# Two-layer cross-attention on one core: scores and row maxima in the two row halves of the TensorE array, maxima issued in pairs of heads

## The chip, the cores and the metric

The kernel runs on one core of a Trainium2 chip. The metric is the device time of one execution in microseconds (us). Engines are named as in the profile: PE is TensorE (PEld its weight loads), DVE is VectorE, ACT is ScalarE, POOL is GpSimd, SP is SyncE, which issues most DMAs here.

## What is computed

Two cross-attention layers are applied one after the other to x of shape (8, 256, 320), with a context of shape (8, 256, 512), 20 heads of 16 columns. The first layer attends to 77 text rows and to the other 179 rows with separate softmaxes and adds the two; the second attends to 252 text rows, and to 4 image rows with a softmax that also contains a cosine term.

```python
# layer 0
q = heads(x @ Wq.T); k = heads(text @ Wk.T); v = heads(text @ Wv.T)
out = attend(q, k, v) + attend(q, k_ip, v_ip)          # softmax(q k / 4) v, twice
x = out @ Wo.T + bo + x
# layer 1
probs_t = softmax(q @ k_t / 4); text_out = probs_t @ v_t
qsem = l2norm(probs_t @ text_ehs); sem = qsem @ l2norm(ip_ehs)
probs_ip = softmax(q @ k_ip / 4 + 0.5 * sem) * spatial_mask
out = (text_out + probs_ip @ v_ip) @ W_out + b_out + x
```

## The kernel before

The work is cut into 16 units: units 0 to 7 are the eight batches in the first layer, 8 to 15 the same in the second. A unit has 10 slots, one for each pair of heads; a slot q = 10 u + j is the unit of the order. `plan(u, j)` lists what happens in a slot, and the programs of all five engines walk the same list, so a table at the top of the file (`PACE`, `MAXH`, ...) sets the order everywhere.

While unit u is attended, two other units are under way: the projections of unit u + 2 ("bg", in three pieces a slot, L388 and L415), and the row maxima of the scores of unit u + 1 ("max", L482), which are needed before its scores can be shifted. A slot holds on TensorE, in this order: the scores of the next pair (L505, two 512-column matmuls, one for each half of the keys), one head of maxima, in even slots the weighing of four heads ("weigh", L537 to L551: four tiles of 32 columns side by side, tile_position (0, 32 j)), in the second layer two quadratic forms ("quad", L519), then the pieces of projection with the other maxima between them, and in even slots four or two transposes ("back", L560). The maxima are dealt three to a slot in slots 0 to 5 and two in slot 6.

Precision is kept by splitting each operand into a rounded high part and a low part. A head has 48 rows in the packed tiles: 16 high, 16 low, 16 high again. In `QP` and `KP` head a of a pair lies in rows 48 a to 48 a + 47; `QP` of a head is zero in the other head's rows, so a maximum contracts over 96 rows (`KROWS`) and the scores over 100 (`QROWS`), the last four being the shift rows (the maxima, high and low) against rows of `ind`. The queries and keys reach these tiles through DRAM (L756, L764), the shift rows by DMAs of one row each (`rows_out`, L780): the high ones from ScalarE's queue in the first layer, the low ones from SyncE's.

PSUM has eight banks. `pPV` is kept for the weighing; the other seven are a pool. `take` gives out, when the program is built, the free bank that was given back first, and makes TensorE wait until whoever reads it is through: VectorE for maxima (dv_mx), for quads (dv_y), for transposes (dv_nb); ScalarE for scores (ac_exp, the exponential at L876); both for projections (ac_bg, dv_bg) and for the transposed output (ac_ot, dv_ot).

ScalarE does, in the order of the list, the rounded exponentials of the scores (second layer, L866), the copy of pPV after a weighing, and the exponentials proper (L876). VectorE reduces each head's maxima (first layer 128x154 and 128x358, second 128x504 and a copy of four columns), multiplies the quads (L1116), computes the low parts (L1001) and normalizes (L1129 to L1147). GpSimd subtracts in the second layer (L1352).

The first slots of units 0 and 1 (`LATE_MAX`) and the slots before unit 0 (u = -1) put the maxima behind the projections.

Of the kernel before, what the change touches and what calls it, by code (L numbers as in the profile page):

```python
# [7 lines left out]
F32 = mybir.dt.float32  # L8
# [6 lines left out]
U = 2 * B  # L15
# [7 lines left out]
KROWS = 96  # L23
QROWS = 100
# [15 lines left out]
MAXH = (3, 3, 3, 3, 3, 3, 2, 0, 0, 0)  # L40
MAXF = (3, 3, 3, 3, 2, 2, 2, 2, 0, 0)
# [40 lines left out]
def plan(u, j):  # L82
# [17 lines left out]
    many = MAXF if u < 0 else MAXH  # L100
    heads = [("max", u + 1, h) for h in range(sum(many[:j]), sum(many[:j + 1]))] if u + 1 < U else []
    first, rest = heads[:1], heads[1:]
# [3 lines left out]
    scores = [("scores", q + 1)] if u >= 0 and q + 1 < U * NP else []  # L106
    weigh = [("weigh", *divmod(q // 2 - 1, NG))] if q >= 2 and q % 2 == 0 else []
    weigh += [("weights", q + 1)] if scores else []
    if u >= B:
        out += scores + weigh + [("quad", q, 0)] + first + [("quad", q, 1)]  # L110
    elif (u, j) in LATE_MAX:
        out += scores + weigh
        rest = heads
    else:
        out += scores + first + weigh
    out += pieces[0] + pieces[1] + rest[:1] + pieces[2] + rest[1:]
# [58 lines left out]
def build(nc, xT, cT, cipT, fs, Wq0, Wk0, Wv0, Wki0, Wvi0, Wo0, bo0,  # L175
          Wq1, Wk1, Wv1, Wki1, Wvi1, Wo1, bo1, ident_d, ind_d, hm_d, outT):
    with ExitStack() as ctx:
# [18 lines left out]
        wk = sb("wk", [128, 2, EC, C], F32R)  # L196
        wv = sb("wv", [128, 2, EC, C], F32R)
# [4 lines left out]
        ind = sb("ind", [4, 2, S], F32R)  # L202
# [12 lines left out]
        P = sb("P", [128, PR, 2, 2 * S])  # L215
        Y = sb("Y", [128, PR, 2, 2 * S])
# [5 lines left out]
        G = [flat(wk)[:, 0:896], flat(wk)[:, 896:1792], flat(wv)[:, 0:896]]  # L222
        PH = [[flat(wv)[:, 896 + 512 * i:896 + 512 * i + 512] for i in range(2)], [flat(w)[:, at:at + 512] for w, at in ((wv, 1920), (wk, 1792))]]
# [25 lines left out]
        Y_flat = Y[:, :, :, :].rearrange("p a b c -> p (a b c)")  # L249
# [16 lines left out]
        def stage(tile, at, n):  # L266
            return flat(tile)[:, at:at + n * C].rearrange("p (k n) -> p k n", n=C)

        sq0, sk0 = stage(Y, 0, KC), stage(Y, KC * C, EC)
        ski0, sv0, svi0 = stage(P, 0, EC), stage(P, EC * C, EC), stage(O2, 0, EC)  # L270
        so0 = stage(Y, 0, KC)
        wki1, wvi1 = stage(Y, 0, EC), stage(Y, EC * C, EC)
        sq1, sk1 = stage(Y, 0, KC), stage(Y, KC * C, EC)
        sv1 = stage(Y, 0, KC), stage(Y, (KC + EC) * C, 1)
# [25 lines left out]
        po_y, po_rn, po_ip, po_set, po_v, po_big, po_q, po_mix = (sem(f"po_{n}") for n in ("y", "rn", "ip", "set", "v", "big", "q", "mix"))  # L300
# [12 lines left out]

        ind_f = flat(P)[0:4, 2 * EC * C:2 * EC * C + S], flat(Y)[0:4, 2 * EC * C:2 * EC * C + S]

        def ind_ready(u):
            u = u if u < 2 else B + u % 2 if u >= B else u % 2
            return l_ind[u], 16

        def rows_landed(u):  # L320
            return l_m[u % 2], 64 * (u // 2 + 1) if u < B else 256 + 32 * ((u - B) // 2 + 1)
# [11 lines left out]
        def tensor_program(_):  # L333
# [142 lines left out]
            def maximum(u, h):  # L476
                i, j, a = u % 2, h // 2, h % 2
                bank = take("mx", u * H + h)
                pe.wait_ge(*pack_landed(u, h // 8))
                pe.wait_ge(po_set, 2 + u % 2)  # L480
                for sc in range(2):
                    made = mm(bank[:, sc * S:sc * S + S], QP[i][0:KROWS, j, a, sc * 128:sc * 128 + 128],  # L482
                              KP[i][0:KROWS, j, :], start=True, stop=True)
                made.then_inc(pe_mx, 1)
                give(bank)
# [191 lines left out]
            for u in range(-1, U):  # L677
# [30 lines left out]
                if u < 0:  # L708
                    scores(0)
# [940 lines left out]
```

## Time and profile before

| | us |
|---|---|
| median of 3 runs | 806.78 |
| lowest, highest | 806.47, 809.67 |
| the profiled execution, its own time | 808.78 |
| its span, first to last instruction | 806.8 |
| busy: PE, DVE, ACT, POOL | 762.5, 567.9, 425.4, 403.0 |
| a unit of the first layer (unit 4, scores of slot 0 to slot 0 of unit 5) | 38.4 |
| a unit of the second layer (unit 11) | 54.8 |

The profile shows one execution. Matmuls are pipelined, so their durations overlap; what one costs is read from the distance between starts. A line of the timeline gives the start, the length and the number of instructions merged in it. Slots are found by their scores (L505): the scores at the head of slot j belong to the pair of slot j + 1.

### The profile page before, as it was taken

How to read it: one execution, taken by the hardware profiler on the slowest of the kernel's cores; microseconds unless marked ns; L12 is line 12 of the kernel's file. 1: busy time of each engine (PE TensorE's matmuls, PEld its weight loads, DVE VectorE, ACT ScalarE, POOL GpSimd, SP SyncE). 2: the span in 40 equal slices, each digit the busy share in tenths (PEclk: the TensorE clock that was granted, in tenths of full speed). 3: DMA queues.
4: the chain of work that ended last, by engine and by line, in shares of the span. 5: the costliest groups of instructions: out<-in, count | busy, mean ns of one | idle time of the engine just before them, and what ended most of it. 6: DMA issues, size and time to landing. Idle time of an engine off the chain costs nothing.

```text
span 806.8 us, 17013 instructions
## 1 busy us (share of the span) xinstructions
PE 762.5 (95%) x6246; PEld 616.4 (76%) x6246; DVE 567.9 (70%) x1575; ACT 425.4 (53%) x915; POOL 403.0 (50%) x297
## 2 busy tenths in 40 slices
PE   5889999999999999999999999999999999988896
PEld 5777788888788877777877778788777787766574
DVE  5357465757576676858768778698697797686745
ACT  5234646464637373646475565555655655555551
POOL 6511222020202040405568887787779778779763
PEclk9999999999999999999999999999999999999999
DMA  9854735654537372735252354153162332400010
GB/s 282 257 165 145 190 111 154 201 169 138 164 113 200 113 202 75 205 94 158 94 146 91 96 144 152 46 157 115 49 190 70 103 118 66 126 1 17 20 34 17
DMA packets 102514, 100.65 MB, mean 125 GB/s; under 512 B 9752, under 2 KB 101664, under 8 KB 102432
## 3 DMA queue, kind: packets, MB, share of 16 engines
q1 hardware_dynamic: 101952, 99.24, 42.2%
q8 instruction: 50, 0.82, 0.4%
q10 hardware_dynamic: 480, 0.33, 0.2%
q14 instruction: 32, 0.26, 0.1%
HBM read 61.65 MB, written 36.74 MB: 122 GB/s over the span
## 4 chain that ended last, share of the span: by engine, by line
PE 71%; DVE 9%; issue 5%; DMA 5%; ACT 4%; POOL 3%; SPq 2%; POOLq 0%; DVEq 0%; ACTq 0%
PE pB L388 19%; PE pB L519 12%; PE pB L482 8%; PE pB L505 7%; PE pB L603 5%; PE pPV L546 4%; PE pPV L541 4%; PE pPV L551 3%; DMA KP<-k0d 3%; PE pPV L537 2%; PE pB L560 2%; POOL Y L1352 2%; DVE m_sb L1101 2%; PE pB L415 1%; ACT P L876 1%
## 5 line engine op out<-in xcount | busy, mean ns | idle before, releaser
L1352 POOL TENSOR_TENSOR Y<-P,wv 128x512 f32<-128x512 f32 x120 | 157.0, 1326 | 106.6 <-ACT P L876 106.5
L1116 DVE TENSOR_TENSOR Y<-pB,Y 128x512 f32<-128x512 f32 x160 | 109.0, 686 | 67.3 <-PE pB L519 56.8
L482 PE MATMUL pB<-KP,QP 96*128 96x256 f32 x640 | 129.1, 287 | 5.0 <-DMA KP<-k0d 3.6
L1329 POOL TENSOR_TENSOR klo<-xin,khi 128x256 fp32r<-128x256 f32 x18 | 13.2, 756 | 232.1 <-ACT khi L787 232.1
L482 PEld LDWEIGHTS pB<-KP,QP 96*128 96x128 f32 x640 | 106.7, 191 | 17.8 <-issue 5.4
L1101 DVE TENSOR_REDUCE m_sb<-pB 128x2 f32<-128x504 f32 x160 | 108.0, 676 | 6.5 <-PE pB L482 5.3
L505 PE MATMUL pB<-QP,KP 100*128 100x512 f32 x320 | 109.8, 422 | 1.9 <-DMA QP<-mlo 1.5
L876 ACT ACTIVATE P<-pB 128x512 f32<-128x512 f32 x160 | 86.5, 597 | 39.5 <-PE pB L505 29.7
L866 ACT ACTIVATE wv<-pB 128x512 fp32r<-128x512 f32 x120 | 66.8, 591 | 67.3 <-PE pB L505 66.0
L876 ACT ACTIVATE P<-pB,ln 128x512 f32<-128x512 f32 x160 | 101.1, 691 | 0.0
L787 ACT ACTIVATE Vs<-pPV 128x512 f32<-128x512 f32 (+1 forms) x80 | 39.3, 492 | 104.7 <-PE pPV L541 71.3
L1099 DVE TENSOR_REDUCE m_sb<-pB 128x2 f32<-128x358 f32 x160 | 83.2, 520 | 0.0
L388 PE MATMUL pB<-cc,wki 128*128 128x256 f32 (+3 forms) x576 | 80.8, 273 | 0.1
L1098 DVE TENSOR_REDUCE m_sb<-pB 128x2 f32<-128x154 f32 x160 | 49.8, 312 | 41.7 <-PE pB L482 41.0
L519 PE MATMUL pB<-wv,wk 128*128 128x512 f32 x250 | 76.7, 410 | 2.5 <-DVE ipS L1103 2.4
L388 PEld LDWEIGHTS pB<-cc,wki 128*128 128x128 f32 (+1 forms) x576 | 70.6, 172 | 6.5 <-issue 4.1
L388 PE MATMUL pB<-wvi,cc 128*128 128x320 f32 (+1 forms) x384 | 68.0, 314 | 1.0 <-POOL wvi L1342 1.0
L388 PE MATMUL pB<-khi,wq 128*128 128x256 f32 (+1 forms) x288 | 56.7, 292 | 9.9 <-DVE wq L1001 8.5
L388 PEld LDWEIGHTS pB<-wvi,cc 128*128 128x128 f32 x384 | 60.0, 190 | 7.1 <-issue 4.5
L1375 POOL TENSOR_TENSOR rn<-n,mhalf 128x8 f32<-128x8 f32 (+2 forms) x17 | 57.1, 3358 | 15.6 <-DVE n L1147 15.6
L519 PEld LDWEIGHTS pB<-wv,wk 128*128 128x128 f32 x250 | 44.3, 189 | 21.1 <-issue 10.3
L505 PEld LDWEIGHTS pB<-QP,KP 100*128 100x128 f32 x320 | 50.8, 191 | 6.3 <-DMA QP<-mlo 2.3
(175 smaller groups left out, 1477.3 us busy)
## 6 DMA issues: line engine op xcount, KB each, us to landing
QP<-q0d SPq DMA_DIRECT2D x64, 192.0 KB, 4.1
KP<-k0d SPq DMA_DIRECT2D x64, 192.0 KB, 4.2
c_sb<-in_cT SPq DMA_DIRECT2D x16, 512.0 KB, 5.3
q0d<-qhi SPq DMA_DIRECT2D x32, 256.0 KB, 2.4
k0d<-khi SPq DMA_DIRECT2D x32, 256.0 KB, 2.4
q0d<-qlo SPq DMA_DIRECT2D x16, 256.0 KB, 2.5
k0d<-klo SPq DMA_DIRECT2D x16, 256.0 KB, 2.5
VB<-vipd SPq DMA_DIRECT2D x6, 640.0 KB, 3.8
```

The source lines that it names most:

```text
L388: made = mm(out, l, r, start=(n == 0), stop=(n == len(pairs) - 1))
L482: made = mm(bank[:, sc * S:sc * S + S], QP[i][0:KROWS, j, a, sc * 128:sc * 128 + 128], KP[i][0:KROWS, j, :], start=True, stop=True)
L505: mm(bank[:, :], KP[i][0:QROWS, j, ch * 128:ch * 128 + 128], QP[i][0:QROWS, j, :, :].rearrange("p a s -> p (a s)"), start=True, stop=True) ...
L519: made = mm(bank[:, :], G[i][:, col:col + 128], ph[src], start=(n == 0), stop=(n == len(jobs) - 1))
L866: act(PH[q % HR][ch], bank_of["sc", q, ch][:, :], ACT.Exp, scale=0.25).then_inc(ac_ph, 1)
L876: act(P[:, q % PR, ch, :], bank_of["sc", q, ch][:, :], ACT.Exp, scale=0.25, **twice).then_inc(ac_exp, 1)
L1098: nc.vector.tensor_reduce(m_sb[:, :, h], v[:, :, 0:TXT0], AX, ALU.max)
L1099: nc.vector.tensor_reduce(m_sb[:, :, H + h], v[:, :, TXT0:S], AX, ALU.max).then_inc(dv_mx, 1)
L1101: nc.vector.tensor_reduce(m_sb[:, :, h], v[:, :, 0:TXT1], AX, ALU.max)
L1116: tt(Y[:, p, dst, :], bank_of["gp", q, dst][:, :], Y[:, p, dst, :], MUL).then_inc(dv_y, 1)
L1352: tt(Y[:, p, ch, :], P[:, p, ch, :], PH[q % HR][ch].bitcast(F32), SUB).then_inc(po_y, 1)
L1375: tt(rn[:, :, hs], n2[:, :, hs], mhalf[:, 0:2 * n].rearrange("p (c h) -> p c h", c=2), POW).then_inc(po_rn, 1)
```

## The change

Head a of a pair now lies in rows 64 a to 64 a + 47 of `QP` and `KP`, the shift rows behind it. A matmul on 48 or 52 rows of one half is built as a tile of 64 rows and 128 columns (tile_size [64, 128]). `maxima(u, j)` issues the maxima of both heads of a pair, alternately in the two halves, into two banks. `scores(q, halves)` does the same in slots that also have maxima and are not late; there a bank holds one head and both key halves instead of one key half and both heads, so the exponentials write through a view. Elsewhere the scores are two full matmuls over 116 rows.

The pairs of maxima stand right behind the scores: 2, 1, 2, 1, 2, 1, 1 in slots 0 to 6. Each halved slot takes two banks for scores and two or four for maxima before the weighing. The shift rows take two DMAs each, one per head. GpSimd's two memsets of the shift rows are replaced by DMAs of `ind`. GpSimd's subtraction waits for both exponentials of a halved slot.

```diff
-KROWS = 96
-QROWS = 100
+KROWS = 48
+QROWS = 52
...
-MAXH = (3, 3, 3, 3, 3, 3, 2, 0, 0, 0)
-MAXF = (3, 3, 3, 3, 2, 2, 2, 2, 0, 0)
+PAIRS = (2, 1, 2, 1, 2, 1, 1, 0, 0, 0)
+PAIRS_FIRST = (2, 1, 2, 1, 1, 1, 1, 1, 0, 0)
...
+    late = u < 0 or (u, j) in LATE_MAX
+    halves = bool(pairs) and not late
...
+    out += scores
+    if halves:
+        out += pairs
+    out += [("weigh", *divmod(q // 2 - 1, NG))] if q >= 2 and q % 2 == 0 else []
+    out += [("weights", q + 1, halves)] if scores else []
     if u >= B:
-        out += scores + weigh + [("quad", q, 0)] + first + [("quad", q, 1)]
...
+        out += [("quad", q, 0), ("quad", q, 1)]
+    out += pieces[0] + pieces[1]
+    if late:
+        out += pairs
+    out += pieces[2]
...
+            def maxima(u, j):
+
+                i = u % 2
+                banks = [take("mx", u * H + 2 * j + a) for a in range(2)]
...
                 for sc in range(2):
...
+                    for a, bank in enumerate(banks):
+                        rows = half(a, KROWS)
+                        made = mm(bank[:, sc * S:sc * S + S], QP[i][rows, j, a, sc * 128:sc * 128 + 128], KP[i][rows, j, :],
+                                  start=True, stop=True)
...
+                    if halves:
+                        for a, bank in enumerate(banks):
+                            rows = half(a, QROWS)
+                            made = mm(bank[:, ch * S:ch * S + S], KP[i][rows, j, ts], QP[i][rows, j, a, :], start=True, stop=True)
...
-                dma(QP[i][r:r + 1, :, :, :].bitcast(F32), tile[h0:h0 + H, :].bitcast(F32)).then_inc(l_m[i], 16)
+                for a in range(2):
+                    row = 64 * a + KROWS + r
+                    dma(QP[i][row:row + 1, :, a, :].bitcast(F32), tile[h0 + a:h0 + H:2, :].bitcast(F32)).then_inc(l_m[i], 16)
...
+                    po.wait_ge(ac_exp, 2 * q + (2 if halves else ch + 1))
...
-                        nc.gpsimd.memset(QP[(u + 1) % 2][KROWS:QROWS, :, :, :].bitcast(F32), 1e20).then_inc(po_big, 1)
```

TensorE, unit 11, slot 4, before: scores (L505), weighing (L546, L551), quads (L519) with a head of maxima (L482) between them. "waits" names what the first matmul waits for.

```order
L505 MATMUL pB3<-QP1,KP1 128x512 [waits dv_y]
L505 MATMUL pB1<-QP1,KP1 128x512 [waits dv_mx]
L546 MATMUL pPV<-P,VY2 32x256 x8
L551 MATMUL pPV<-Y,y21 32x256 [waits dv_y]
L551 MATMUL pPV<-Y,y21 32x256 x7
L519 MATMUL pB0<-wv 128x512 [waits ac_ph]
L519 MATMUL pB0<-wv 128x512 x3
L482 MATMUL pB5<-KP0,QP0 128x256 [waits dv_mx]
L482 MATMUL pB5<-KP0,QP0 128x256
L519 MATMUL pB2<-wv 128x512 [waits dv_bg,ac_bg]
L519 MATMUL pB2<-wv 128x512 x2
```

The same place now: scores (L522), two pairs of maxima (L492), weighing (L569, L574), quads (L542).

```order
L522 MATMUL pB0<-QP1,KP1 128x256 [waits dv_mx,ac_exp]
L522 MATMUL pB2<-QP1,KP1 128x256
...
L492 MATMUL pB6<-KP0,QP0 128x256 [waits dv_y,dv_mx]
L492 MATMUL pB3<-KP0,QP0 128x256
...
L492 MATMUL pB5<-KP0,QP0 128x256 [waits dv_bg,ac_bg,dv_y]
L492 MATMUL pB1<-KP0,QP0 128x256
...
L569 MATMUL pPV<-P,VY2 32x256 x8
L574 MATMUL pPV<-Y,y21 32x256 x8
L542 MATMUL pB0<-wkv 128x512 [waits ac_ph,ac_exp]
L542 MATMUL pB0<-wkv 128x512 x3
L542 MATMUL pB2<-wkv 128x512 [waits ac_exp]
```

The quads now go to pB0 and pB2, the banks of the scores at the head of this slot, and the second pair goes to banks whose reader is the low part of a key projection (dv_bg).

TensorE, unit 4, slot 2, first layer, now: scores, two pairs of maxima, weighing (L560). Before, the bank that waits for the transposed output (dv_ot, ac_ot) was taken by the last head of maxima of the slot, behind weighing and projections.

```order
L522 MATMUL pB1<-QP0,KP0 128x256 [waits dv_mx,ac_exp]
L522 MATMUL pB2<-QP0,KP0 128x256
...
L492 MATMUL pB5<-KP1,QP1 128x256 [waits dv_bg,ac_bg,dv_mx]
L492 MATMUL pB6<-KP1,QP1 128x256
...
L492 MATMUL pB3<-KP1,QP1 128x256 [waits dv_ot,ac_ot,l_ld11,dv_bg,ac_bg]
L492 MATMUL pB4<-KP1,QP1 128x256
...
L560 MATMUL pPV<-P,VX 32x256 [waits dv_fix]
```

That wait now stands ahead of the weighing.

## Rows read from the trace of the kernel before

**Rows 1.** The page: busy time and instructions, granted clock, chain by engine.

```profile
PE 762.5 (95%) x6246; PEld 616.4 (76%) x6246; DVE 567.9 (70%) x1575; ACT 425.4 (53%) x915; POOL 403.0 (50%) x297
...
PEclk9999999999999999999999999999999999999999
...
PE 71%; DVE 9%; issue 5%; DMA 5%; ACT 4%; POOL 3%; SPq 2%; POOLq 0%; DVEq 0%; ACTq 0%
```

**Rows 2.** TensorE's waits: us in total, times, longest.

```profile
PE pB L388 <- DVE wq L1001: 8.5, 1, 8.5
PE pB L560 <- ACT Vs L787: 4.7, 4, 2.8
```

**Rows 3.** Groups by line and shape, TensorE and ScalarE: busy us, mean ns, idle before.

```profile
L482 PE MATMUL pB<-KP,QP 96*128 96x256 f32 x640 | 129.1, 287 | 5.0 <-DMA KP<-k0d 3.6 <-ACT P L876 0.6 <-DVE m_sb L1099 0.6
L505 PE MATMUL pB<-QP,KP 100*128 100x512 f32 x320 | 109.8, 422 | 1.9 <-DMA QP<-mlo 1.5 <-DVE qlo L1001 0.2
...
L546 PE MATMUL pPV<-P,VY 128*32 128x256 f32 x640 | 42.8, 385 | 0.0
...
L876 ACT ACTIVATE P<-pB,ln 128x512 f32<-128x512 f32 x160 | 101.1, 691 | 0.0
```

**Rows 4.** Timeline of unit 11, slot 2: start us, length us, operation, count.

```profile
541.91 0.63 PE L505 MATMUL pB<-QP,KP 100*128 100x512 f32 x2
...
542.46 1.07 PE L546 MATMUL pPV<-P,VY 128*32 128x256 f32 x16
...
543.35 1.05 PE L551 MATMUL pPV<-Y,y 128*32 128x256 f32 x16
...
544.33 1.21 PE L519 MATMUL pB<-wv 128*128 128x512 f32 x4
...
544.88 0.34 ACT L896 ACTIVATE ex<-t 128x160 f32<-128x160 f32 x1 [2.76 <-DVE t L1159]
...
545.38 0.41 PE L482 MATMUL pB<-KP,QP 96*128 96x256 f32 x2
...
545.62 0.86 PE L519 MATMUL pB<-wv 128*128 128x512 f32 x3
...
546.08 0.39 ACT L787 ACTIVATE Vs<-pPV 128x256 f32<-128x256 f32 x1
...
546.33 1.11 PE L388 MATMUL pB<-cc,wki 128*128 128x256 f32 x8
546.34 1.28 ACT L876 ACTIVATE P<-pB,ln 128x512 f32<-128x512 f32 x2
...
547.28 0.40 PE L482 MATMUL pB<-KP,QP 96*128 96x256 f32 x2
```

**Rows 5.** Engines in one window, slots 0 to 6 of unit 11; busy us by engine.

```profile
core 0: us, PE busy (x) PEld busy (x) DVE busy (x) ACT busy (x) POOL busy (x), PEclk, DMA share, GB/s
531.00:571.00 40.00, 39.16 (x323) 31.03 (x321) 34.14 (x93) 20.60 (x43) 33.74 (x25) 1.00 0.44 129
```

**Rows 6.** Timeline of unit 11, slot 4.

```profile
552.68 0.63 PE L505 MATMUL pB<-QP,KP 100*128 100x512 f32 x2
...
553.62 0.67 DVE L1001 TENSOR_TENSOR klo<-pB,khi 128x504 fp32r<-128x504 f32 x1
```

**Rows 7.** Timeline of unit 4, slots 1 and 2, first layer.

```profile
218.12 0.46 PEld L573 LDWEIGHTS pB<-ident,O 128*128 128x128 f32 x4
...
218.58 0.72 PE L505 MATMUL pB<-QP,KP 100*128 100x512 f32 x2
...
218.86 0.60 ACT L787 ACTIVATE ahi<-pB 128x512 fp32r<-128x512 f32 x1 [0.88 <-PE pB L573]
...
219.66 0.68 DVE L1001 TENSOR_TENSOR alo<-pB,ahi 128x512 fp32r<-128x512 f32 x1
```

**Rows 8.** Timeline of ScalarE and its DMA queue, unit 4, slot 7.

```profile
241.26 1.52 ACTq L780 DMA_DIRECT2D QP<-mhi  x2
242.84 1.08 ACT L876 ACTIVATE P<-pB 128x512 f32<-128x512 f32 x2 [1.60 <-issue]
```

More of the change, by code:

```diff
@@ L99, in plan @@
         pieces = [[], [], []]
-    many = MAXF if u < 0 else MAXH
-    heads = [("max", u + 1, h) for h in range(sum(many[:j]), sum(many[:j + 1]))] if u + 1 < U else []
-    first, rest = heads[:1], heads[1:]
+    many = PAIRS_FIRST if u < 0 else PAIRS
+    pairs = [("max", u + 1, jj) for jj in range(sum(many[:j]), sum(many[:j + 1]))] if u + 1 < U else []
+    late = u < 0 or (u, j) in LATE_MAX
+    halves = bool(pairs) and not late
     out = []
@@ L105, in plan @@
         out += [("shift", u + 1)]
-    scores = [("scores", q + 1)] if u >= 0 and q + 1 < U * NP else []
-    weigh = [("weigh", *divmod(q // 2 - 1, NG))] if q >= 2 and q % 2 == 0 else []
-    weigh += [("weights", q + 1)] if scores else []
-    if u >= B:
-        out += scores + weigh + [("quad", q, 0)] + first + [("quad", q, 1)]
[L111 to L116, printed above, removed]
+    scores = [("scores", q + 1, halves)] if u >= 0 and q + 1 < U * NP else []
+    out += scores
[3 more added lines that the diff above has]
+    out += [("weights", q + 1, halves)] if scores else []
+    if u >= B:
+        out += [("quad", q, 0), ("quad", q, 1)]
[3 more added lines that the diff above has]
+    out += pieces[2]
     if q >= 2 and q % 2 == 0:
@@ L474, in prepare @@
                     give(bank)
[L476 to L480, printed above, removed]
-                for sc in range(2):
[L482 to L485, printed above, removed]
+            def maxima(u, j):
+                i = u % 2
+                banks = [take("mx", u * H + 2 * j + a) for a in range(2)]
+                pe.wait_ge(*pack_landed(u, j // 4))
+                pe.wait_ge(po_set, 2 + i)
+                for sc in range(2):
+                    for a, bank in enumerate(banks):
+                        rows = half(a, KROWS)
+                        made = mm(bank[:, sc * S:sc * S + S], QP[i][rows, j, a, sc * 128:sc * 128 + 128], KP[i][rows, j, :],
+                                  start=True, stop=True)
+                        if sc == 1:
+                            made.then_inc(pe_mx, 1)
+                for bank in banks:
+                    give(bank)
             def shift_rows(u):
@@ L495, in shift_rows, with scores @@
                 give(bank)
-            def scores(q):
+            def scores(q, halves):
                 u, j = divmod(q, NP)
@@ L708, in tensor_program @@
                 if u < 0:
-                    scores(0)
+                    scores(0, False)
             weigh(U - 1, NG - 1)
```

141 lines of the change are left out of this document (79 added, 62 removed).

## The prediction

> **What bounds the kernel now.** I read first the busy times, the granted clock and the chain of work that ended last [rows 1]. TensorE is busy for 95% of the span at a clock of 0.989, and 71% of the chain is its own work; VectorE has 70%, ScalarE 53%, GpSimd 50%. So matmul time is on the path nearly everywhere, and the list of what TensorE waited for says the same: after one start-up wait of 8.5 us the next item is 4.7 us in four waits [rows 2]. Then the groups: the maxima (L482, 640 matmuls of 256 columns) and the scores (L505, 320 of 512 columns) [rows 3]. Their mean durations (287 and 422 ns) overlap, so the price is the distance from start to start, from a stretch of the timeline [rows 4]: three 512-column matmuls take 545.62 to 546.33, 0.236 us each (other stretches 0.232), eight of 256 columns 546.33 to 547.28, 0.118 each.
>
> VectorE is less idle than its 70%: in slots 0 to 6 of a second-layer unit (531.0 to 571.0) it is busy 34.1 of 40.0 us [rows 5]. That matters, because all maxima lie in these slots and TensorE waits for a bank until VectorE or ScalarE has read it.
>
> **The change, part by part.** *Array work.* Two matmuls in the two row halves should run at once. No row shows row halves. The nearest are the weighings, four column tiles: 16 matmuls of 385 ns mean [rows 3] start within 542.46 to 543.35 [rows 4], 0.22 us for each four. So four tiles do run together, loads included, and I take one round of two halves as one matmul, 0.118. Maxima: 640 x 0.118 = 75.5 become 320 rounds, 37.8: -37.8 us. Scores are halved only in slots that have pairs and are not late, 15 x 7 - 2 = 103: 206 x 0.232 = 47.8 becomes 206 x 0.118 = 24.3: -23.5. Sum -61.3. The other end for a round is twice 0.115, were the two loads of 128 columns to queue: four such loads in a row take 0.46 [rows 7]. That is the third case below. Below 0.118 it can't go, since 256 columns stream in that time in any row.
>
> *Changes of tiling.* The visits to column tiles price them [rows 4]: L505 to L546 is 0.55 for two 512s (0.464), so 0.09 to enter. Out: L551 to L519 is 0.98 for four rounds of 0.215, so 0.12, and the four matmuls that follow take 1.05 where 4 x 0.232 is 0.93, 0.12 more, since the first load hides behind nothing. A change between whole array and halves thus costs 0.21. There are 113 visits to the halves (103 and 10 late ones), 23.7 us. From 58 of them TensorE goes on to a weighing, whose entry it paid before; 55 go back to the whole array, 11.6. Were the first load hidden after all, entries would be 0.09, 14 us less. Sum of both parts: -61.3 + 35.3 = **-26.0**.
>
> *New waits.* Four maxima in a row plus two score banks plus a projection bank are all seven banks, so whatever follows takes a bank that was written this very slot. The order shows it: the first quad of slots 2 and 4 now waits for the exponential of the scores at the head of the same slot, where before it waited for nothing of that kind.
> In slot 2 (start 541.91) ScalarE does ex at 544.88 because VectorE is late with it, then two rounded exponentials and the copy of pPV, then the exponential from 546.34 [rows 4], which takes 0.69 [rows 3]. VectorE's share of that isn't sped up, so the quad may start about 4.9 us into the slot; TensorE would be free at 0.9 (scores, pairs) + 0.1 + 1.9 (weighing) = 2.9. Wait: 2.0.
> In slot 4 (start 552.68) the second pair waits for klo, which ended 554.29, 1.6 in [rows 6], while it is wanted at 0.7: 0.9. Then the weighing, the copy (0.26 to the next start) and the exponential follow in a chain, 1.05 more before the quad. Queued behind these waits on TensorE are the weighing, the quads and the projections. With 0.4 for VectorE being behind, 0.3 for the second pair of slot 2 and 0.35 in slot 0, a unit gains 5.0 us of waits. What goes: the unit holds 1.5 us over its matmul time now (40.0 against 38.5 by these prices). Net +3.5, five folded units (9 to 13): +17.7; units 8 and 14 I take at half, +3.5.
> In the first layer the second pair of slot 2 waits for alo: 218.58 to 220.34 is 1.76 [rows 7], wanted at 0.7, 0.9 with the slot before shortened. The projection bank of slot 4 waits for the exponential behind copy and weighing, 0.5; slot 0 0.5, slot 2's last bank 0.2. The hi rows leave ScalarE by four issues instead of two; two take 1.52 and the exponentials wait 1.60 for them [rows 8]. SyncE's lo rows double too. With 1.5 more on each, I take 0.7 of it as seen, at the scores of the next unit. 2.8 x 7 units = +19.6.
> At the least these waits are the bare chains: 1.6 a unit in the first layer, 2.95 - 1.5 in the folded ones (1.05 in slot 2, 0.9 and 1.05 in slot 4), 1.5 for units 8 and 14, together 20.
>
> *Edits at nothing.* Loads to rows 64 and up and the merged weights tile move the same bytes. GpSimd loses two memsets (L1413); it has half its time idle [rows 1]. GpSimd's first subtraction waits for both exponentials, 0.6 later; its result is wanted a slot later, over 3 us of cover. If that were gone it would cost 0.6 a slot.
>
> *Sum*: -26.0 + 19.6 + 17.7 + 3.5 = **+14.8**. The profiled run took 808.8 (span 806.8), the median is 806.8, 0.2% less; so 806.8 + 14.8 = 821.6, 821.
>
> **Rivals.** *The waits stay small, faster.* With the bare chains the sum is -26.0 + 20 = -6, with hidden first loads -20: 787 to 801. For it: TensorE waits so little now that the banks have slack, and VectorE has 5.9 us of idle time in the 40. Against: the order's dependence, and that the exponential follows a weighing that stands behind the pairs. The point from which it decides: net new waits of 26.0 / 14 = 1.9 us a unit, over seven units of each layer.
> *The halves don't run together, slower still.* The change then doesn't do what it says. At 0.23 a round the 526 rounds cost 59 us more than at 0.118, of which the new waits hide up to half: 851 to 880.
> *Dead heat*: waits between the bare ones and mine, 803 to 810.
>
> The Trainium skill, "TensorE: Matmul & The Clock Gate", Part 3, says that loads overlap running matmuls only where the row groups differ, and reports four row tiles of 32 rows at 3.07 times the speed of one. No run here shows row tiles. By that 3.07 of 4 a round would be an estimated 0.154, and the sum 526 x 0.036 = 19 higher, 840. It speaks against the third case and for a smaller gain than mine.
>
> **How the numbers follow.** Forecast (halves run together, waits of my size): 0.45. Faster: 0.31. Dead heat: 0.12. Halves not together: 0.12. Range 790 to 846: it takes in the bare chains without most of the hidden loads, the forecast with waits half as large again (+20, 841), and leaves out the third case and the very best. About 0.5% is what a measurement can tell from no change. Faster by more 0.31, within 0.12, slower 0.45 + 0.12 = 0.57. The likeliest case alone is 812 to 841.
>
> **What would show it.** Right: two halved matmuls start within some 10 ns and the next two 0.118 later; 0.09 to 0.12 at each change; new waits of TensorE at the quad for the exponential (P) and at the maxima for klo and alo, 2 us a time in units 9 to 13; PE busy below 90%. Wrong: rounds 0.23 apart (third case); quads that start right behind the weighing (faster); maxima that wait for Y or ipS for microseconds, with VectorE busy over 95% of slots 0 to 6 (a bound I priced at 0.4 a unit only).

## The result and the profile after

| | us |
|---|---|
| kernel before, median of 4 (lowest, highest) | 808.22 (806.47, 809.96) |
| changed kernel, median of 4 (lowest, highest) | 860.44 (854.53, 864.50) |
| ratio, 95% interval | 1.0636, 1.0597 to 1.0675 |
| span of the profiled run, before and after | 806.8, 862.6 |

The change costs 52 us. The forecast was 821 with a range to 846: the sign was right, the size was not.

The page of the changed kernel, busy time and granted clock, beside [rows 1]:

```profile
PE 759.5 (88%) x6452; PEld 586.5 (68%) x6452; DVE 573.7 (67%) x1575; ACT 425.4 (49%) x915; POOL 394.5 (46%) x295
...
PEclk9989899999999999999999999999999999999999
```

TensorE is busy for 759.5 us, about as long as before (762.5). The 55.8 us that the span grew by are idle time, and clock: the mean granted clock fell from 0.989 to 0.968. The groups of maxima and halved scores, beside [rows 3]:

```profile
L492 PE MATMUL pB<-KP,QP 48*128 48x256 f32 x640 | 68.0, 298 | 46.0 <-DMA KP<-k0d 22.0 <-DVE klo L1030 9.9 <-DVE alo L1030 7.4
L522 PE MATMUL pB<-QP,KP 52*128 52x256 f32 x412 | 52.5, 333 | 0.0
```

The maxima's busy time is 68.0 us where it was 129.1: two halves do run together. But 46.0 us of idle time stand right before them, where there were 5.0. The list of TensorE's waits (us in total, times, longest), beside [rows 2]:

```profile
PE pB L492 <- DMA KP<-k0d: 22.0, 13, 3.0
PE pB L542 <- ACT P L905: 18.3, 14, 2.5
PE pB L492 <- DVE klo L1030: 9.9, 8, 2.0
PE pB L395 <- DVE wq L1030: 8.4, 1, 8.4
PE pB L492 <- DVE alo L1030: 7.4, 8, 1.7
```

The second, third and fifth are waits that the prediction named. The first, for the keys of the next unit, it did not. In unit 11, slot 0, the timeline reads:

```profile
562.82 0.51 PE L522 MATMUL pB<-QP,KP 52*128 52x256 f32 x4
...
566.19 1.04 PE L492 MATMUL pB<-KP,QP 48*128 48x256 f32 x8 [2.87 <-DMA KP<-k0d]
...
567.16 1.93 PE L569 MATMUL pPV<-P,VY 128*32 128x256 f32 x16
...
568.86 1.53 PE L574 MATMUL pPV<-Y,y 128*32 128x256 f32 x16
...
570.32 2.13 PE L542 MATMUL pB<-wkv 128*128 128x512 f32 x7
```

The maxima could follow the scores at about 563.2 (562.82 and 0.34 for the two rounds of scores), and start at 566.19. SyncE issues the keys' load behind the output's DMAs of the previous unit, about 2 us ahead of slot 0, in both kernels. The rows of SyncE and of the first maximum before:

```profile
529.08 1.27 SPq L764 DMA_DIRECT2D KP<-k0d  x2
...
534.48 0.40 PE L482 MATMUL pB<-KP,QP 96*128 96x256 f32 x2
```

and of SyncE now:

```profile
560.77 1.28 SPq L787 DMA_DIRECT2D KP<-k0d  x2
```

By the trace's semaphores the second of the two DMAs landed 3.0 us into slot 0 before and 3.2 us now. The load is no later; its reader is: it stood 3.45 us into the slot (531.03 to 534.48), and now asks for the keys after 0.34. The weighing and the quads stand behind the maxima. Then something else shows: the four rounds of L569 take 1.70 us (567.16 to 568.86), where [rows 4] has four in 0.89. The granted clock of that stretch and of one in slot 2 is the column behind the engines (x gives the number of instructions):

```profile
566.00:569.60 3.60, 3.41 (x32) 1.95 (x36) 3.14 (x9) 0.00 (x0) 1.54 (x2) 0.56 1.07 235
577.00:580.50 3.50, 3.16 (x42) 2.38 (x44) 3.37 (x8) 0.98 (x2) 2.53 (x3) 1.00 0.57 199
```

TensorE idled for 2.9 us, and was then granted 1.2 GHz instead of 2.4 for most of the first stretch. Slot 2 of the same unit:

```profile
578.05 0.50 PE L522 MATMUL pB<-QP,KP 52*128 52x256 f32 x4
...
578.39 0.40 PE L492 MATMUL pB<-KP,QP 48*128 48x256 f32 x4
...
579.13 0.50 PE L492 MATMUL pB<-KP,QP 48*128 48x256 f32 x4 [0.34 <-DVE qlo L1030]
...
582.28 1.28 ACT L905 ACTIVATE P<-pB,ln 128x512 f32<-128x512 f32 x2
...
583.03 1.89 PE L542 MATMUL pB<-wkv 128*128 128x512 f32 x7 [1.54 <-ACT P L905]
```

This is the wait the prediction worked out: the quad starts 4.98 us into the slot (forecast 4.9), right behind the first exponential.

Where the 55.8 us lie, by the distances between the first scores of the units in both traces:

| part | forecast | measured |
|---|---|---|
| start, units 0 and 1 | +1.0 | +8.4 |
| units 2 to 7 | +5.6 | +11.8 |
| units 8 to 14 | +8.2 | +35.5 |
| unit 15 and the end | 0 | +0.1 |

(The forecast column is the prediction's sum shared out: -1.86 a unit of array work, +2.8 of waits in the first layer, the second layer's waits as given.)

### The profile page after: what moved, and what is told of

It reads as the page before. It is cut to its first block and busy times, and to the rows that moved or that the text cites. A ratio compares the mean times of both kernels' runs of the same rounds, so it can differ in the third digit from the quotient of the medians.

```text
span 862.6 us, 17634 instructions
## 1 busy us (share of the span) xinstructions
PE 759.5 (88%) x6452; PEld 586.5 (68%) x6452; DVE 573.7 (67%) x1575; ACT 425.4 (49%) x915; POOL 394.5 (46%) x295
## 5 line engine op out<-in xcount | busy, mean ns | idle before, releaser
L1384 POOL TENSOR_TENSOR Y<-P,wkv 128x512 f32<-128x512 f32 x160 | 207.6, 1320 | 147.7 <-ACT P L905 147.3
L542 PE MATMUL pB<-wkv 128*128 128x512 f32 x560 | 155.3, 414 | 19.5 <-ACT P L905 18.3
L1146 DVE TENSOR_TENSOR Y<-pB,Y 128x512 f32<-128x512 f32 x160 | 106.7, 686 | 72.4 <-PE pB L542 62.7
L542 PEld LDWEIGHTS pB<-wkv 128*128 128x128 f32 x560 | 101.7, 192 | 64.9 <-ACT P L905 27.3
L895 ACT ACTIVATE wkv<-pB 128x512 fp32r<-128x512 f32 x160 | 86.3, 592 | 76.5 <-PE pB L522 57.4
L492 PE MATMUL pB<-KP,QP 48*128 48x256 f32 x640 | 68.0, 298 | 46.0 <-DMA KP<-k0d 22.0
L492 PEld LDWEIGHTS pB<-KP,QP 48*128 48x128 f32 x640 | 49.8, 188 | 55.9 <-issue 40.4
L395 PE MATMUL pB<-cc,wki 128*128 128x256 f32 (+3 forms) x576 | 77.3, 278 | 1.5 <-ACT P L905 1.5
L395 PEld LDWEIGHTS pB<-cc,wki 128*128 128x128 f32 (+1 forms) x576 | 68.3, 174 | 11.3 <-issue 4.1
L395 PEld LDWEIGHTS pB<-khi,wq 128*128 128x128 f32 (+1 forms) x288 | 44.5, 187 | 16.4 <-DVE wq L1030 8.4
L522 PE MATMUL pB<-QP,KP 52*128 52x256 f32 x412 | 52.5, 333 | 0.0
```

Of the source, the lines that this page charges most:

```text
L395: made = mm(out, l, r, start=(n == 0), stop=(n == len(pairs) - 1))
L492: made = mm(bank[:, sc * S:sc * S + S], QP[i][rows, j, a, sc * 128:sc * 128 + 128], KP[i][rows, j, :], start=True, stop=True)
L522: made = mm(bank[:, ch * S:ch * S + S], KP[i][rows, j, ts], QP[i][rows, j, a, :], start=True, stop=True)
L542: made = mm(bank[:, :], G[i][:, col:col + 128], ph[:, src, :, :].rearrange("p a s -> p (a s)"), start=(n == 0), stop=(n == len(jobs) - 1))
L895: act(split(PH[q % HR], n, halves), scored(q, n), ACT.Exp, scale=0.25).then_inc(ac_ph, 1)
L1146: tt(y, bank_of["gp", q, dst][:, :], y, MUL).then_inc(dv_y, 1)
```

## The experiments

All times below are medians, and the ratios are to runs of the kernel before on the same chip. Lengths of slots are distances between first scores. Two moves are tried against the changed kernel, each alone and together: slot 0's pairs late, and the second pair of double slots late. A kernel that keeps the order but takes the halves away, and one that fills the wait, go with them.

**Whole array, same order (x_full).** Ratio 1.0851 (1.0813 to 1.0889), 876.4 us. The maxima of 12 units read the shift rows too, so their results are shifted and only the time counts.

```diff
-    halves = bool(pairs) and not late
+    first = bool(pairs) and not late
+    halves = False
...
-    if halves:
+    if first:
         out += pairs
...
-                        rows = half(a, KROWS)
+                        rows = slice(0, 64 + KROWS) if u not in (0, 1, B, B + 1) else half(a, KROWS)
```

> Order of the changed kernel, tiles as before: every scores matmul spans both row halves (two of 512 columns a slot), and the maxima of units 2 to 7 and 10 to 15 span rows 0 to 111 (those of units 0, 1, 8 and 9 stay in the halves). The full maxima read the shift rows too, so their results are shifted; the time is what counts. By the prices of the prediction's rows (0.118 a matmul of 256 columns, 0.232 one of 512) the array work grows by 12 x 20 x 0.118 = 28.3 for the maxima and 103 x 0.228 = 23.5 for the scores, and about 84 of the 113 visits to the halves go, 84 x 0.21 = 17.6 back: +34 where TensorE is what is waited for. Theory (the order of the list costs the time: maxima wait for keys and for banks, and the work behind them with them): the waits stay, only part of them is filled, 865 to 890. Rival (the halves themselves are dear: mode changes or two loads at once cost more than I priced): it falls towards the kernel before, 805 to 830.

So the halves are no loss: without them the same order is 16 us slower (17 by the ratios), not faster. The rival (dear halves) falls, and the loss is the order's. The expected +34 leaves out the way back to the whole array of the 36 visits that no weighing follows; with it (36 x 0.21 = 7.6) the same prices give about 26. The four largest waits (for the keys, P, klo and alo) sum to 50.7 us here and to 57.6 in the changed kernel, so part of the added work filled waits.

**Slot 0 late (x_slot0); second pairs late (x_second); both (x_both).**

```diff
-    late = u < 0 or (u, j) in LATE_MAX
+    late = u < 0 or (u, j) in LATE_MAX or (u >= B - 1 and j == 0)
```

```diff
     if halves:
-        out += pairs
+        out += pairs[:1]
...
-    if late:
-        out += pairs
+    out += pairs if late else pairs[1:]
```

> Only change against the changed kernel: in slot 0 of units 7 to 14 the two pairs of maxima stand behind the projections, as in slot 0 of units 0 and 1, and the scores there are whole. Theory (in the second layer these maxima wait for the keys' load, 22.0 us in 13 waits, and TensorE's clock is granted at half after some of them): the waits for KP fall below 8 us in all, slot 0 of units 9 to 13 goes back from 7.3 to 11.3 us to about 7, and the time falls by 15 to 25, to 836 to 846. Rival (the wait only hides one for VectorE, which reads the maxima, or for ScalarE's exponentials; it moves to the quads): falls by less than 6.

> Against the changed kernel only the second pair of slots 0, 2 and 4 moves behind the second piece of projection; the first pair of slot 0 keeps waiting for the keys. So far: with slot 0 late alone 858.1, with both 821.7. Theory (the second pair is nearly the whole of it: it takes the banks whose readers are not through, and the quads get the banks of this slot's scores): slots 2 and 4 of units 10 to 13 take 7.4 and 6.8 us instead of 8.5 and 8.4 to 12.1, slots 0 and 1 together about 0.9 more than with slot 0 late, 824 to 834. Rival (both moves are needed, as long as one wait per unit is left TensorE's clock falls): 838 to 850.

> As x_slot0, and in the other slots with two pairs (2 and 4 of every unit, slot 0 of the first layer's) only the first pair stands behind the scores, the second behind the second piece of projection, in the halves too: about 37 more visits from and to the whole array, at 0.2 each +7.5 us. Theory (four maxima in a row take the last free banks, so the quads wait for the exponential, 18.3 us in 14 waits, and the second pair for klo and alo, 17.3 in 16): these waits nearly go, slots 2 and 4 of units 9 to 13 come back from 8.5 to about 6.7, a further 18 to 30 below x_slot0, net of the visits: 806 to 825. Rival (VectorE and ScalarE are the bound in these slots, wherever the maxima stand): no better than x_slot0, 836 to 850.

| | second pairs early | second pairs late |
|---|---|---|
| slot 0 early | 860.4, ratio 1.0636 | 836.9, 1.0350 (1.0312 to 1.0389) |
| slot 0 late | 858.1, 1.0621 (1.0577 to 1.0665) | 821.7, 1.0158 (1.0112 to 1.0204) |

Slots 0 to 6 of unit 13, us:

| kernel | 0 | 1 | 2 | 3 | 4 | 5 | 6 |
|---|---|---|---|---|---|---|---|
| before | 6.6 | 4.3 | 6.5 | 4.3 | 6.3 | 5.2 | 6.8 |
| changed | 8.8 | 3.9 | 8.5 | 3.9 | 8.4 | 4.5 | 6.0 |
| slot 0 late | 6.9 | 4.9 | 8.9 | 3.9 | 11.1 | 4.5 | 6.0 |
| second pairs late | 10.9 | 3.9 | 7.2 | 3.9 | 6.7 | 4.4 | 6.0 |
| both | 6.9 | 4.9 | 7.4 | 3.9 | 6.8 | 4.4 | 6.0 |

The moves don't add up. Slot 0 late gains 2 us alone and 15 with the other: the theory of that run (15 to 25 less), that the 22 us of waits for keys are worth their length, was wrong there. Its trace shows why. The wait for KP fell to 8.2 us, and slot 0 came back to 6.9. But slot 1 grew by 1.0, because its pair now waits for VectorE, which reads the maxima of slot 0 later:

```profile
685.62 0.50 PE L522 MATMUL pB<-QP,KP 52*128 52x256 f32 x4
686.70 0.50 PE L492 MATMUL pB<-KP,QP 48*128 48x256 f32 x4 [0.58 <-DVE ipS L1132]
687.27 1.88 PE L542 MATMUL pB<-wkv 128*128 128x512 f32 x7
```

and slot 4 of units 10, 12 and 13 took 10.9, 12.1 and 11.1 us, where the changed kernel has 8.4 in all three: a stretch at half clock now falls there. (In unit 11 it is the other way round, 8.4 instead of 11.1.) With the second pairs late alone it is slot 0 that pays for both, 10.9 us in unit 13. The same slot of unit 12:

```profile
605.92 0.50 PE L521 MATMUL pB<-QP,KP 52*128 52x256 f32 x4
608.58 0.50 PE L491 MATMUL pB<-KP,QP 48*128 48x256 f32 x4 [2.15 <-DMA KP<-k0d]
609.01 1.94 PE L568 MATMUL pPV<-P,VY 128*32 128x256 f32 x16
610.72 1.89 PE L573 MATMUL pPV<-Y,y 128*32 128x256 f32 x16
612.54 1.89 PE L541 MATMUL pB<-wkv 128*128 128x512 f32 x7
```

A wait of 2.15 us, then the eight rounds of the weighing in 3.53 us (609.01 to 612.54) instead of 1.87 [rows 4]. In this slot the wait and the half clock behind it cost about the same, 2.2 and 1.7 us.

The second pair is the larger cause. Late, it brings slots 2 and 4 from 8.5 and 8.4 to 7.2 and 6.7 us; the waits of quads for P (18.3 us) and of maxima for klo and alo (17.3) are gone from its list of waits, where 6.1 us of maxima waiting for P have come in. Alone it lies between what its theory (824 to 834) and the rival (838 to 850) expected, and with slot 0 late too the time, 821.7, is inside the expected 806 to 825.

**Filling the waits (x_warm, w_warm).** Useless matmuls before the waits, the order untouched: eight before the keys' wait, then also two or four before the second pairs.

```diff
+                if u > B and j == 0:
+                    for _ in range(8):
+                        mm(banks[0][:, :], wki[:, 0, 0, 0:128], wki[:, 0, 1:3, 0:256], start=True, stop=True)
                 pe.wait_ge(*pack_landed(u, j // 4))
```

> Against the changed kernel: before the wait for the keys in slot 0 of units 8 to 14, eight matmuls of 512 columns (1.9 us at full clock) into the bank of the first maximum, overwritten by it. They fill the wait of 1.7 us on average with work that nobody needs. If the granted clock of 0.5 after these waits costs time of its own, slots 0 lose their long weighing rounds (0.41 instead of 0.215) and the time falls by 5 to 12, to 848 to 855. Rival (the half clock hides behind the other engines' chain, or comes from other waits): no change or up to 6 us slower, where the dummies outlast the wait.

> Against the changed kernel, useless matmuls fill its waits without moving anything: eight of 512 columns before the keys' wait in slot 0 (as x_warm), four before the second pair of slot 2 in the first layer and of slot 4 in the second, two before that of slot 2 in the second, into pPV, which is free there. The waits of the quads stay empty. If the half clock is a cost of its own, the time granted at 0.5 falls from 54.6 us to below 35 and the time by 8 to 14, to 846 to 852. If the falls only shift to the quads' waits, it stays within 4 of x_warm (856.6).

856.6 us (1.0602, 1.0549 to 1.0656) and 855.4 (1.0538, 1.0491 to 1.0584). In the second kernel the clock of 500 to 760 us is whole, where the changed kernel had 0.97. The windows, w_warm first, the changed kernel behind:

```profile
500.00:760.00 260.00, 243.66 (x1963) 183.57 (x1961) 198.25 (x505) 131.75 (x277) 185.48 (x125) 1.00 0.35 100
```

```profile
500.00:760.00 260.00, 230.19 (x1868) 174.82 (x1866) 193.34 (x498) 131.25 (x275) 185.08 (x123) 0.97 0.36 101
```

Units 11 to 13 took 180.1 us instead of 183.6. So work that nobody needs can be worth its time where the clock would fall. Over the whole run that isn't shown. The first kernel's gain is 0.3%, within the intervals. The second's is 1.0% by the ratio (8 us; 5 by the medians), and the intervals don't overlap; but in the two profiles it does not lie where the useless work stands. Unit 0, which has none of it, took 35.0 us instead of 41.4 and unit 1 took 41.8 instead of 44.1; the changed kernel ran 13.7 us of these two units at half clock, the other none. From slot 0 of unit 2 to slot 0 of unit 15 w_warm took 659.6 us and the changed kernel 657.0. So these units have less half clock (20.5 us instead of 27.3) and no less time.

Both expected times were missed, 848 to 855 and 846 to 852; the second kernel lies within 4 us of the first, as its rival had it. What the half clock costs in all, and what the useless work costs where it outlasts a wait, stays open.

**The keys earlier (z_keys, and with the second pairs late z_second_keys).** The other way to take the wait away, one line of SyncE's program:

```diff
+                        if j == 7:
+                            load_keys(sp, dma, u + 2, 0)
                         if j == 8:
-                            load_keys(sp, dma, u + 2, 0)
```

> Against the changed kernel one line of SyncE's program moves: the load of the next but one unit's first keys is issued in slot 7, behind the shift rows, and no longer in slot 8, behind the output's DMAs (in unit 11 it was issued at 560.77 and landed at 566.19, while the maxima stood ready at 563.3). Nothing else is touched, so this takes the wait away where x_slot0 put other work in its place. Theory (the wait is worth its length, but in x_slot0 slot 1 grew by 1.0, slot 2 by 0.4, and three units lost 2.5 us each to the half clock in slot 4): KP waits fall from 22.0 to below 5, slot 0 of units 9 to 13 takes 6.6 to 7.2, 840 to 850. Rival (the wait only moves to the next bank, as it seemed with slot 0 late): 855 or more.

> The second pairs late (836.9) and the keys' load in slot 7. Theory (what is left in that kernel is the wait for the keys, 18.7 us in 10 waits, and TensorE's half clock behind it, 71 us at 0.5 against 33 in the kernel with slot 0 late): both go, slots 0 and 1 of units 10 to 13 take 6.6 and 3.9 against 6.9 and 4.9 there, 804 to 814, level with the kernel before. Rival (VectorE and the exponentials hold these slots however the keys come): as with slot 0 late, 819 to 825.

851.3 us, ratio 1.0526 (1.0469 to 1.0584), and with the second pairs late 815.3, 1.0104 (1.0048 to 1.0159). Alone the move lands between its two expectations: KP waits fell to 9.2 us, not below 5, slot 0 of units 10 to 13 takes 7.4 to 7.5, and slot 4 of units 11 and 12 takes 12.1 where the changed kernel has 11.1 and 8.4. With the second pairs late slots 0 and 1 of unit 13 are 6.8 and 4.0 us (expected 6.6 and 3.9), and units 10 to 13 take 54.1 each: at least 0.7 less than before the change. The expected 804 to 814 was missed by 1.3.

The waits that are left lie in the first layer and at the start. In the first layer the reader did not move: before, too, the first maximum stood right behind the scores of slot 0. The load did. In SyncE's queue it stands behind the shift rows' DMAs, which are now four instead of two. Ahead of slot 0 of unit 3 (171.93 before, 181.94 now), before:

```profile
166.19 1.63 SPq L780 DMA_DIRECT2D QP<-mlo  x2
167.87 1.26 SPq L764 DMA_DIRECT2D KP<-k0d  x2
```

and in the changed kernel:

```profile
175.81 3.14 SPq L803 DMA_DIRECT2D QP<-mlo  x4
179.00 1.25 SPq L787 DMA_DIRECT2D KP<-k0d  x2
```

The keys' load is issued 2.9 us ahead of the slot instead of 4.1, and its second DMA lands 1.6 us into the slot instead of 0.2 us ahead of it. In z_keys it stands behind the same four and is issued 3.0 us ahead, which is why the move brings nothing there. (The reason given with w_best, that the keys are stored late, is not what the trace shows: their stores are issued over 10 us ahead of the slot, and SyncE does not pause between the shift rows and the load.)

**All pairs late (x_late), slot 0 late everywhere (y_s0all), other dealings (y_alt, z_mix, z_mix_odd).**

> Against the changed kernel all pairs stand behind the second piece of projection and all scores are whole matmuls over both halves: only the maxima are in the halves. Array work by the prediction's prices: 103 x 0.228 = 23.5 us more than with halved scores, 2 visits to the halves the fewer where a slot had split ones. If TensorE's own time is what is left once the waits are gone, this is 15 to 24 above the kernel with slot 0 and the second pairs late (821.7): 836 to 846. If VectorE, which reads all maxima in slots 0 to 6, holds these slots, the scores' half costs little: 821 to 832.

842.7 us (1.0421, 1.0394 to 1.0447), inside the expected 836 to 846, but not for the reason given: the last pair of slot 6 stands right before the shift rows' transposes, which wait 7.8 us for ipS and 5.3 for m_sb (4.3 and 3.0 before the change), and slot 6 takes 7.4 us instead of 6.0.

> As the kernel with slot 0 of units 7 to 14 and the second pairs late (821.7), but slot 0 late in all units: in the first layer the maxima of slot 0 no longer wait for the keys' load (in units 2 to 6 slot 0 took 6.2 to 9.3 us against 4.8 to 6.1 in the kernel before). Theory: slots 0 of units 2 to 6 come to about 5.5, 4 to 7 us in all less, 814 to 818. Rival (what these maxima wait for is passed to the next slot, as in the second layer, where slot 1 grew by 1.0): within 2 of 821.7.

> As the kernel before in this list (slot 0 late everywhere, second pairs late), but the pairs dealt one, two, one, two, one, two, one. With two, one, two, ... VectorE is busy 4.90 of 5.0 us in slot 1 and 3.76 of 3.9 in slot 3 of unit 11, while TensorE has 4.36 and 3.90. Theory (VectorE holds the odd slots): a pair costs it 1.4 us, so slots 1, 3 and 5 of units 9 to 13 grow by 1.0 to 1.4 each and slots 0, 2 and 4 shrink by 0.3 to 0.8: +2 us a unit, 830 to 840. Rival (only TensorE's order matters; odd slots have less array work, so the load is more even): 808 to 818.

819.5 us (1.0143, 1.0105 to 1.0180) and 820.8 (1.0121, 1.0070 to 1.0173): no difference between the two that can be told. The late slot 0 in the first layer gains 2.2 us by the medians and 1.2 by the ratios, within the noise: it mostly passes its wait on, as its rival said. The theory that VectorE's share of a single slot decides (830 to 840) falls, and the even load gained less than its rival expected (808 to 818); units 10 to 13 take 54.7 with the odd dealing, 55.1 with the other. Slots 0 to 6 of unit 13 take 39.8 us with the odd dealing and 40.2 with the other: what one slot has more its neighbours have less.

> Keys' load in slot 7; in the second layer the second pairs late as in z_second_keys, in the first layer both pairs stand behind the scores and are dealt two, one, one, two, two, one, one, so that no double slot falls on slot 2, where the second pair waited 1.2 us for alo. Theory (in the first layer each split double slot costs a visit of 0.38 and no quads wait there): about 0.8 us a unit less than z_second_keys over seven units, 5 us, 799 to 809. Rival (slots 3 and 4 in a row with two pairs run out of banks, VectorE reads them too late): 2 to 8 above z_second_keys.

> As z_mix, but in the second layer the pairs are dealt one, two, one, two, one, two, one (units 10 to 13 took 54.7 us with this dealing and slot 0 late, 55.0 with two, one, two). Theory: the same within 4 us of z_mix, since both dealings cost the same visits. Rival (slot 0 needs the second pair early, its VectorE work falls on slots 1 and 3): 5 to 10 above.

820.2 (1.0153, 1.0108 to 1.0198) and 822.6 us (1.0165, 1.0117 to 1.0214): 5 us above z_second_keys, in the rival's range, though the intervals overlap; the theory (799 to 809) falls. The other dealing is the same within 4 us, as expected. In the first layer two double slots in a row take 3.5 and 6.9 us where 2.2 and 6.7 stood, the second pairs waiting for ahi (5.1 us in six waits).

**What the halves are worth when hardly anything waits (w_whole_scores, w_all_whole).** Both kernels start from z_second_keys; the edits are those of the first experiment, scores alone and then maxima too.

> Against z_second_keys (815.3, hardly any waits left) only the scores are whole matmuls again, two of 512 columns for 103 slots that had four halved ones; the number of visits to the halves stays. Theory (with the waits gone TensorE's time is the bound, and the prediction's price of the scores, 103 x 0.228 = 23.5 us, holds): 833 to 841. Rival (VectorE and the exponentials hold the slots, so the array work that the halves save is not on the path): 816 to 824.

> As w_whole_scores, and the maxima of units 2 to 7 and 10 to 15 span rows 0 to 111 too (they read the shift rows, so their results are shifted; the time is what counts): the order of z_second_keys almost without halves. Maxima +28.3 us by the prediction's prices; in those 12 units ten visits each go, six with the whole array on both sides (0.38 each in the traces) and four with a weighing behind (0.19): 3.0 x 12 = 36.5 back. Theory (a visit for one pair alone costs more than the pair saves): 8 us below w_whole_scores, 826 to 833, and 15 above z_second_keys. Rival (visits are cheaper than this when nothing waits, the halves gain their full 28.3): 10 or more above w_whole_scores.

825.7 us (1.0165, 1.0135 to 1.0195) and 825.9 (1.0172, 1.0140 to 1.0205). Halves for the scores are worth 0.6% or 5 us by the ratios, at the edge of the noise, and not 23.5 (the rival's 816 to 824 is met by the ratio, 822, and missed by the median). Halves for the maxima bring nothing on top that can be told: neither the 8 us below w_whole_scores that the theory had nor the rival's 10 above. By the distances in unit 13, halved scores take 1.6 us of work out of slots 0 to 6, as the prediction priced them (seven times 0.23), but the slots get only 0.4 shorter: the second pair of slot 2 waits 0.6 us for an exponential (P) instead of 0.2, and three more short waits, of 0.1 to 0.3 us, appear, the longest for VectorE's ST. An odd slot shows the exchange. With halves (z_second_keys, unit 13, slot 1, from the last transposes to the projections):

```profile
650.40 0.39 PE L582 MATMUL pB<-ident,Vs 128*128 128x128 f32 x2
650.72 0.50 PE L521 MATMUL pB<-QP,KP 52*128 52x256 f32 x4
651.06 0.40 PE L491 MATMUL pB<-KP,QP 48*128 48x256 f32 x4
651.47 1.89 PE L541 MATMUL pB<-wkv 128*128 128x512 f32 x7
653.19 0.65 PE L394 MATMUL pB<-khi,wq 128*128 128x256 f32 x4
```

Whole (w_all_whole):

```profile
660.58 0.38 PE L583 MATMUL pB<-ident,Vs 128*128 128x128 f32 x2
660.72 0.71 PE L527 MATMUL pB<-QP,KP 116*128 116x512 f32 x2
661.27 0.64 PE L492 MATMUL pB<-KP,QP 112*128 112x256 f32 x4
661.75 1.78 PE L542 MATMUL pB<-wkv 128*128 128x512 f32 x7
663.36 0.65 PE L395 MATMUL pB<-khi,wq 128*128 128x256 f32 x4
```

Scores and maxima take 0.75 us instead of 1.03, but the two transposes before them 0.32 instead of 0.14, and the seven quads behind 1.72 instead of 1.61: 2.79 against 2.78 in all. A lone pair between projections costs 0.15 more in halves than whole (648.82 to 649.92, against 659.17 to 660.12). Only the even slots gain, 0.27 us (scores and pair 0.68 instead of 1.04, less 0.09 before them), where a weighing follows whose entry is paid anyhow. Slots 0 to 6 of unit 13 take 39.1 us with halves and 39.7 without.

**The best orders (w_best, w_last).**

> As z_second_keys, with slot 0 late in units 0 to 6, where the maxima still wait 1.2 to 1.5 us for the keys (their transposed text part is stored late). Units 2 to 6 took 38.2 each that way, 42.0 for unit 6. Theory: 1 to 4 below z_second_keys, 811 to 815, still not below the kernel before. Rival (start and end, where TensorE runs at the half clock, vary by more than that): no difference.

> As w_best, but the keys' load is issued in slot 7 only from unit 8 on (in all seven profiles with the earlier load the first scores start at 57.8 to 60.2 us, in the others at 55.5 to 57.0), and slot 0 is late up to unit 8 (there it took 9.6 us with the first pair early, 7.2 late). Theory: 2 to 4 us at the start and 1.4 in unit 8 come back, 806 to 811, a ratio of 0.998 to 1.003 to the kernel before: level, with 0.7 us a unit gained in units 10 to 13 and lost again at the start and in units 6, 7 and 14. Rival (start and end vary from run to run whatever the load does): the ratio stays at 1.005 or above.

814.4 us (1.0057, 1.0027 to 1.0088) and 812.9 (1.0031, 1.0004 to 1.0059). The first lies in its expected 811 to 815, but its interval overlaps that of z_second_keys, so the rival (no difference) isn't excluded. The second missed its 806 to 811 by 2 us and its ratio (0.998 to 1.003) by a hair; its rival, 1.005 or above, lies over the measured ratio but inside the interval. The start did come back: the first scores stand at 57.8 to 60.2 us in seven profiles with the earlier load, at 55.2 in w_last. So the best order found is 0.3% above the kernel before, with an interval that ends just short of level. w_last issues the keys early only from unit 8 on:

```diff
+                        if j == (7 if u >= B else 8):
+                            load_keys(sp, dma, u + 2, 0)
                         if j == 8:
-                            load_keys(sp, dma, u + 2, 0)
```

## Why the prediction was right and wrong

*Two halves run together: right.* In the trace the second matmul of a round starts 0 to 12 ns after the first, mostly 3 or 4, and the next round 0.11 to 0.12 us later; in 78 of the 320 rounds of maxima, such as the second round behind a wait, the two are 25 to 55 ns apart. The Trainium skill, "TensorE: Matmul & The Clock Gate", Part 3, gives 3.07 for four row tiles, which made an estimated 0.154 a round; the trace has full concurrency of two, so the measurement decides against that estimate.

*Prices of tile changes: right.* From the last whole matmul to the first halved one is 0.21 where two whole ones stand 0.118 apart, and the first round lasts 0.22 instead of 0.12: 0.19 to enter, and as much to leave. Forecast: 0.21. The Trainium skill, "TensorEngine Tiling (Array Packing)", Key Properties, says that switching the tiling mode drains TensorE; the trace agrees, with these 0.19 us.

*Array work -26.0: right in the trace, if read without waits.* By the distances between starts, slots 0 to 6 of unit 13 hold 6.9 us of waits in 43.9 us, so 37.0 of work; before, 1.2 in 39.9, so about 38.8. That is -1.8 a unit against the forecast's -1.86 (26.0 shared out over 14).

*Waits in slots 2 and 4: right.* In unit 13 the quads wait 1.62 us in slot 2 (forecast 2.0) and 1.15 in slot 4 (1.05); the second pair 0.50 and 1.04 (0.3 and 0.9); VectorE's lateness adds 0.37 (0.4). The first layer has 1.1 us for alo in slot 2 (0.9). (Five units at +3.5 are 17.5, where the sum has 17.7.)

*Slot 0: the step that failed.* The sum has "0.35 in slot 0" for the second layer and "slot 0 0.5" for the first. It was 2.1 us in unit 13 and 1.4 in unit 3, and slot 0 is longer by 17.0 us in units 10 to 14 together, half clock included, and by 5.1 in units 2 to 7. I had asked of each moved group which bank it takes, and of slot 0 too. I had not asked when the data comes that it reads. In the second layer the first maximum had stood behind scores, weighing and a quad, 3.45 us into the slot, in unit 11 0.4 us behind the landing of its keys; the change put it "right behind the scores", and the prediction did not look at the landing of the load that feeds it, though DMA KP<-k0d stood in [rows 3] as the largest reason for idle time at L482 (3.6 us in all, 2.5 of it once at the start). In the first layer it is the other step, "SyncE's lo rows double too. With 1.5 more on each, I take 0.7 of it as seen, at the scores of the next unit": the 1.5 us are right (3.14 instead of 1.63), but the keys' load stands behind these rows, so they are seen at the maxima of slot 0, 0.9 to 1.3 us in each of units 2 to 8.

*The clock: not in the sum at all.* The prediction read 0.989 and took it as given. The mean went to 0.968: 862.6 x 0.968 against 806.8 x 0.989 is 37 us of full-speed time more for 56 us of span, so the clock can account for at most 19. How much of that it did cost stays open: the filled waits shortened units 11 to 13 by 3.5 us and units 2 to 14 not at all.

*Units 0 and 1: +8.4, not forecast.* Scores waited for the shift rows, once for 3.5 us, where [rows 3] has 1.5 in all:

```profile
PE pB L527 <- DMA QP<-mlo: 4.1, 2, 3.5
```

The doubled row DMAs alone don't cost this much: z_keys has them too, in the same order, and its profile shows 76.2 us for these two units, none at half clock, where the changed kernel's has 85.5 with 13.7 at half clock and the kernel before 78.2 with none. Why the clock fell there in one profile and not in the other no run shows.

*Waits don't add.* The forecast summed them per place. The two-by-two table shows -2, -24 and -39 where a sum of the first two would be -26: with slot 0 late alone, part of the time came back as a wait for VectorE in slot 1 and as half clock in slot 4.

*The rivals.* The case in which the waits stay small is what z_second_keys comes near to, and even there the time is 1% above before, not 1 to 2% below: of the -26 the late second pairs take 16 (three more visits in each of 14 units, 0.19 each way), and part of the rest turns into waits for the exponential and for VectorE, as the comparison with w_whole_scores shows. The third case, halves one after the other, is excluded by the starts; that its number, 851 to 880, holds the result is chance.

## What to carry to other kernels

When a group of instructions moves forward, ask two things of it: which buffers it takes from those behind it, and when its own input lands. The second cost 2.1 us here in a slot for which 0.35 was put down. And when DMAs are added to a queue, look at which load stands behind them, not only at who reads them. Tiles of part of the array gain little in ones and twos: with a change of tiling at 0.19 us each way, a visit must save more than three rounds of 0.118, or stand next to work that is tiled already. And when the busiest engine gets less to do, its waits for the others grow: the Trainium skill ("Trainium Kernel Development and Optimization", Best Practices) says that TensorE tiling doesn't speed up PSUM evacuation, and the trace agrees: in slots 0 to 6 of unit 11 VectorE was busy 34.1 of 40.0 us before [rows 5], and 34.6 of 40.1 in z_second_keys.

## What the runs showed of the hardware

- In the changed kernel waits for keys of 2.87, 2.25 and 2.79 us, in an otherwise busy stretch (slot 0 of units 11, 12 and 14), were each followed by a granted clock of 0.5; waits of 1.90 and 1.92 us (units 10 and 13) were not. In x_second waits of 1.70 and 1.91 us (units 10 and 14) were. So the length of a wait alone did not decide it: slot 0 of unit 13 took 8.8 us, that of unit 11 took 11.3. Without slot 0's wait, half-clock stretches fell on slot 4 of units 10, 12 and 13 instead.
- Filling waits with useless matmuls took units 2 to 14 from 27.3 to 20.5 us at half clock, and from 657.0 to 659.6 us in time.
- The same two units of the same order (0 and 1) had 13.7 us at half clock in one profile and none in another, 85.5 and 76.2 us.
- Two matmuls on 48 rows in the two row halves start mostly 3 or 4 ns apart, and a round of them takes 0.12 us, as long as one on 112 rows.
- Four DMAs of shift rows instead of two took SyncE's queue 3.14 us instead of 1.63; the keys' load behind them was issued 2.9 us ahead of its slot instead of 4.1 (unit 3).
